# A decoder's plain attention stages: layernorm moments one step later on VectorE, and exponentials ahead of the stacked copies on ScalarE

## The reference, cut to what matters

```python
Q, K, V = query @ Wq + bq, ctx @ Wk + bk, ctx @ Wv + bv     # 16 heads of 8 (in L2f: 4 of each head's 8 are used)
scores  = einsum('bhqd,bhkd->bhqk', Q, K) * scale           # L3x: masked keys
attn    = softmax(scores, axis=-1)
out     = einsum('bhqk,bhkd->bhqd', attn, V) @ Wo + bo
x       = _layernorm(x + out)                               # (x - mean) / sqrt(var + 1e-5)
```

## Time and profile before

| what | us |
|---|---|
| median of 3 runs | 1776.23 |
| lowest and highest run | 1766.54, 1776.57 |
| the profiled execution | 1782.28 |
| its span | 1780.5 |
| L1x, first to last maximum | 574.7 to 711.8 |
| L2f, first to last maximum | 1188.6 to 1319.6 |
| L3x, first to last maximum | 1568.6 to 1707.1 |

### The profile page before, as it was taken

How to read it: one execution, slowest core, us unless ns; L and a number is a source line. 1 busy time by engine, 2 the same in 40 slices (tenths; PEclk the granted TensorE clock), 3 DMA queues, 4 the chain that set the end, 5 groups by cost and what they waited for, 6 DMA issues and landing times.

```text
span 1780.5 us, 34673 instructions
## 1 busy us (share of the span) xinstructions
PE 1553.0 (87%) x12802; PEld 1109.2 (62%) x12812; DVE 1278.3 (72%) x2840; ACT 1071.1 (60%) x2213; POOL 676.6 (38%) x769
## 2 busy tenths in 40 slices
PE   6688779899998888889999999998889999988875
PEld 5344447678877554667777766665549984755542
DVE  2688862687776887479999567658754449668887
ACT  4489932366765675399999155547654443146755
POOL 3455515578885012356767313220000112501223
PEclk9799989899999997989898999999989999799985
DMA  3200121200000000010000100000000000000000
GB/s 130 109 13 13 42 85 38 58 11 1 1 1 1 1 2 1 4 36 1 1 1 1 58 2 2 2 13 1 2 1 1 1 6 5 1 19 1 2 1 24
DMA packets 14791, 30.94 MB, mean 17 GB/s; under 512 B 1537, under 2 KB 10145, under 8 KB 13857
## 3 DMA queue, kind: packets, MB, share of 16 engines
q1 hardware_dynamic: 13602, 26.63, 4.3%
q0 software_dynamic: 1024, 2.10, 0.4%
HBM read 22.42 MB, written 6.29 MB: 16 GB/s over the span
## 4 chain that ended last, share of the span: by engine, by line
PE 48%; DVE 18%; ACT 12%; POOL 12%; issue 10%; DMA 0%; SPq 0%; DVEq 0%; POOLq 0%; ACTq 0%
PE PS L1344 6%; DVE negmax L2722 5%; PE PS L1404 5%; POOL big L820 4%; PE PS L1664 3%; PE PS L1675 3%; POOL big L808 3%; ACT big L2190 3%; PE PS L1426 2%; POOL big L816 2%; PE PS L1840 2%; ACT big L2168 2%; PE PS L1349 2%; PE PS L1824 2%; PE PS L1319 1%
## 5 line engine op out<-in xcount | busy, mean ns | idle before, releaser
L2168 ACT ACTIVATE big<-PS 128x1024 f32<-128x1024 f32 (+1 forms) x256 | 248.2, 971 | 174.5 <-PE PS L1355 173.6
L2722 DVE TENSOR_REDUCE negmax<-PS 128x4 f32<-128x1024 f32 x192 | 235.0, 1224 | 70.6 <-PE PS L1344 69.5
L704 POOL TENSOR_TENSOR rstd<-veps,mhalf 128x2 f32<-128x2 f32 x72 | 51.2, 712 | 402.1 <-DVE veps L2596 401.6
L1344 PE MATMUL PS<-KS,QS 32*128 32x256 f32 (+1 forms) x1152 | 136.8, 323 | 52.8 <-DVE negmax L2722 37.7
L1344 PEld LDWEIGHTS PS<-KS,QS 32*128 32x128 f32 x1152 | 88.9, 191 | 132.1 <-DVE negmax L2722 89.6
L1404 PE MATMUL PS<-big,V 128*32 128x256 f32 (+1 forms) x2048 | 140.8, 395 | 0.7 <-ACT big L2168 0.4
L1355 PE MATMUL PS<-QS,KS 32*128 32x256 f32 (+1 forms) x1152 | 136.8, 325 | 1.0 <-ACT big L2168 0.9
L730 POOL TENSOR_TENSOR res<-resb,XB 128x256 f32<-128x256 f32 x24 | 17.4, 726 | 289.8 <-ACT resb L2254 289.8
L772 POOL TENSOR_SCALAR KT<-QT 128x1024 f32<-128x1024 f32 x64 | 66.6, 1040 | 67.4 <-DVE QT L2741 65.4
L2741 DVE SCALAR_TENSOR_TENSOR QT<-PS,wint 128x1024 f32<-128x1024 f32 x64 | 77.3, 1220 | 18.6 <-PE PS L1297 17.8
L1355 PEld LDWEIGHTS PS<-QS,KS 32*128 32x128 f32 x1152 | 86.7, 191 | 5.1 <-issue 3.7
(11 more groups left out here) (463 smaller groups left out, 4345.4 us busy)
## 6 DMA issues: line engine op xcount, KB each, us to landing
W<-in_wpack SPq DMA_DIRECT2D x1, 4180.0 KB, 13.9
W<-in_wpack SPq DMA_DIRECT2D x1, 2560.0 KB, 8.9
W<-in_wpack SPq DMA_DIRECT2D x1, 2449.5 KB, 8.2
y_rows<-one_more SPq DMA_DIRECT2D x1, 2048.0 KB, 9.1
masks<-in_mask SPq DMA_DIRECT2D x8, 256.0 KB, 2.8
x_rows<-x_tok SPq DMA_DIRECT2D x16, 128.0 KB, 2.2
W<-in_wpack SPq DMA_DIRECT2D x1, 1538.0 KB, 6.0
x_tok<-in_x SPq DMA_DIRECT2D x1, 1024.0 KB, 5.0
```

Of the source, the lines that this page charges most:

```text
L1344: mm = nc.tensor.matmul(PS[:, MAXB[half], o], QS[r, bm % 2, tm, j * P:(j + 1) * P], KS[r, bm % 2, tm, k], start=not a.causal, stop=last)
L2168: nc.scalar.activation(PX[:, T % 2, 2 * p:2 * p + 2, 0:cols], PS[:, exp_banks(g)[0]:exp_banks(g)[0] + 2, 0:cols], ACT.Exp, scale=a.scale). ...
L2722: ins = nc.vector.tensor_reduce(negmax[:, h:h + 2, :].rearrange("p h j -> p (h j)"), banks.rearrange("p h (j k) -> p (h j) k", j=2), AX.X, ...
```

## The change

In the plain attentions the exponentials of a step are issued on ScalarE ahead of that step's `stack`, instead of behind it. The moments of a batch are taken at `a.y_at + 2` (step 6 of the round) instead of `a.y_at + 1` (step 5), for the steps up to 64. For the last two batches (`g` of 69 and 77) they stay at `a.y_at + 1`. The rotary stage keeps both as they were. No instruction is added or removed.

```diff
@@ ScalarE, turned_steps
                         if (b := due(g, a.project_at + (-1 if a.rope else 1))) is not None:
                             high(b)
+                        if not a.rope and 0 <= g - a.lag < PAIRS * B:
+                            exponentials(g - a.lag)
                         for u in range(2):
                             if (b := due(g, a.unit_at[u] + 1)) is not None:
                                 stack(b, u)
-                        if 0 <= g - a.lag < PAIRS * B:
+                        if a.rope and 0 <= g - a.lag < PAIRS * B:
                             exponentials(g - a.lag)
@@ VectorE, turned_steps
                     if a.pool_tail:
-                        if (b := due(g, a.y_at + 1)) is not None:
+                        first_moments = due(g, a.y_at + 1) if a.rope or g > PAIRS * B else due(g, a.y_at + 2)
+                        if (b := first_moments) is not None:
                             dve.wait_ge(sem("t_sum"), at("t_sum", b + 1))
```

## The result

The changed kernel takes 1752.58 us (median of 4 runs, 1750.87 to 1755.34), the kernel before 1776.40 beside it (4 runs). The ratio is 0.9882, with a 95% interval from 0.9845 to 0.9918. Run once more on another chip the change took 1753.62, the kernel before 1775.78, ratio 0.9892 (0.9856 to 0.9928). The forecast was 1770.6, range 1758 to 1781. Ratios are taken between runs that stood next to each other, so they are not the quotient of the two medians.

The account below looks back on a forecast made before the run. A round was taken as a chain over three engines, none of them full, with the moments delaying step 5. Gains of 3.1 (L1x), 2.5 (L3x) and 0 (L2f) made 5.6 us: 1776.2 to 1770.6, range 1758 to 1781.

Parts of the forecast that it names:

- 0.51 a round in L1x: L1x rounds 2 to 6 each end 0.51 us earlier, round 7 gains 0.57: 3.1 us for the stage.
- 0.39 in L3x: L3x full rounds with moments each end 0.39 us earlier, the last gains 0.57: 2.5 us for the stage.
- nothing in L2f: L2f, where only ScalarE's order changes: 0, between a gain of 0.6 us and a loss of 2.6.
- 0.80 us to the next scores: L1x, TensorE: the scores of step 6 follow `unit` by 0.80 us, loading at 653.65 instead of 653.55.
- L2f's loss at the full clock: L2f: `add_bias` goes behind the copies and `turn_shift` waits for it, a loss of 0.4 us a round.
- The bill that was named: L1x step 5: `turn_shift` waits for the later `copy_y`, loading at 652.48 instead of 652.17.
- The clock: TensorE's falls from 2.4 to 1.2 GHz, costed at nothing because they can go either way.
- Rival 1: Clock falls in L1x and L3x go with the moments' stall: 8.5 us more than the sum, 1762; chance 0.19.
- the price worked out behind that rule: Less TensorE idling in step 5 would bring fewer clock falls, making the sum about 1762 us.
- Rival 2: Moments cost in step 6 all they cost in step 5: 1776 us, 1778 with L2f's loss; chance 0.18.
- Rival 3: Slower: the clock falls ahead of the last round in both L1x and L3x, +5.1 us, 1781; chance 0.13.

Follow-up runs that it names:

- the experiment with reads first: The change with L2f's old ScalarE order and the read of y ahead of the stacked copies in L1x and L3x: 1754.07 us, ratio 0.9895 against the kernel before.

## Why the prediction was wrong

**The steps were about right.** The forecast counted 5.6 us: 0.51 a round in L1x, 0.39 in L3x, nothing in L2f. Measured at the full clock: 0.65 and 0.71, 8.1 with the two last rounds, less 0.3 x 5 = 1.5 in L2f, and less 0.2 each in rounds 0 and 1 of L1x and of L2f, which were costed at nothing: 6.2. That the sum came out so near is in part luck, since its errors cancel. In L1x `unit` was given 0.80 us to the next scores, a spacing read in step 3; but there the maximum held the scores (it starts at 648.18, and they load 1.29 us later). In the change the scores of step 6 follow `unit` by 0.56 (648.27 to 648.83) and load 0.11 us after the exponential behind the read of y ends. In L3x the same spacing, with the mask's matmuls added to it, made the round 16.49 where 16.17 came. And L2f's loss at the full clock, which the text put at 0.4 and then netted to nothing, is 0.3 a round. The bill that was named, `turn_shift` waiting for `copy_y`, shows in the trace, but the experiment with reads first shows that it costs nothing of its own.

**The step that failed is "The clock".** It said: "I cost this at nothing in the sum: it can go either way." It went one way, and was the larger part: 42 us less at the half clock over the runs, worth 17 us. With the moments' stall open in every round, rounds 2 to 7 of L1x ran 10 to 23 us at the half clock in the profiles, with the stall gone or filled 0 to 3.4. Filling the stall alone is worth a ratio of 0.9927 (13 us), twice what the steps are worth. Rival 1 described this, and got a chance of 0.19 and a price of 8.5 us, which is still too small.

**Why it was set too low.** L2f was taken as evidence against: it falls without such a stall. But L2f shows only that falls have other causes as well, not that this stall is none. The case for was in plain sight: 1.72 us of idle weight loads in each round of L1x and L3x, and a fall just behind it in round 7. The list of falls was also short by one: round 2 of L3x took 18.12 us at clock 0.91, where 16.88 is a round at 1.00. The rule of the Trainium skill that was named beside rival 1 ("TensorE: Matmul & The Clock Gate", Part 1: The HAM clock gate: activity releases the throttle) is borne out by the fillers in L1x and L3x, which add activity and shorten no step (ratio 0.9927). By the price worked out behind that rule the time would have been 1762; it was 1752.58.

**What stays open.** 17 us from the clock and 4 (by the means above) to 6 (by the rounds) from the steps make 21 to 23 us, near what the ratios have (0.9882 and 0.9892, 19 to 21 us; 23.8 and 22.2 between the medians). How much of the 17 is the stall's is not shown. The filler's share is 13 us by its ratio, but its two stages alone add up to 6, and the moments alone, which close the stall and shorten the rounds as well, have the same median as the filler (1758.51). The two parts of the change gain 10 and 2 us alone and 19 to 21 together. Falls in unchanged stages also differ between the first two profiles (10.4 us outside the three attentions), and nothing run here shows whether the change has a part in that.

**The other rivals.** Rival 2 (no net gain in the steps) is refuted by rounds of 16.00 and 16.17. Rival 3 (a fall ahead of the last round in both stages) is the opposite of what came: no profile with the stall gone has one in L1x or L3x.

## What to carry to other kernels

When a change closes a regular gap of TensorE, price the clock as a part of the gain and not as noise around it: compare the same round at 1.00 and below, and see whether the fall follows the gap. Filler matmuls in the gap are a cheap test, since they shorten no step. Compare the granted clock of all runs too, and not that of one profile, which may be an extreme of its kernel. Moving one copy ahead of another on a queue that is full over two steps only changed who waits here; the queue's sum stayed.

## What the runs showed of the hardware

More work made the kernel faster: 96 matmuls that nobody reads (8 in each of 6 rounds of two stages) brought a ratio of 0.9927, with 31 us less at 1.2 GHz. Over 80 runs of one kernel the span grew by 0.40 us for each us at 1.2 GHz. Round 7 of L1x stayed at 1.2 GHz from its start to its end (19.78 us) in the kernel before and in the one with the exponentials alone, while the same round ran at 2.4 GHz in 13.79 to 14.42 us in 11 of the other 12 profiles: nothing in it brought the clock back. And the kernel before is wide: on one chip from 1753 us, at a granted clock of 0.943, to 1784, at 0.925.
